# Value bias folded into other biases, value copies on ScalarE, low half of the scaled input by a negative identity, remote part transposed from its bank

## What is computed

```python
qkv = x @ qkv_w + qkv_b;  q, k, v = split(qkv)
local = windowed_attention(q, k, v)                   # 16 heads of 16, window of 128 earlier tokens
pooled = x.reshape(B, 64, 8, D).mean(2)               # 64 latent tokens
rq = x @ rq_w + rq_b;  rk, rv = split(pooled @ rkv_w + rkv_b)
lat_out = masked_attention(rq, rk, rv)                # 4 heads of 16, only earlier chunks
remote = lat_out @ rout_w + rout_b
gate = sigmoid(local @ gl_w + remote @ gr_w)          # one number per token and head
mixed = gate * local + (1 - gate) * remote
x = layernorm(x + mixed @ out_w + out_b)
h = gelu(rms_norm(x) @ ternary(w_up).T)
x = layernorm(x + rms_norm(h) @ ternary(w_down).T)
```

## Time and profile before

| what | us |
|---|---|
| runs shown, median (lowest, highest) of 3 | 1172.92 (1170.47, 1173.93) |
| the profiled execution, its time | 1173.3 |
| its span, first to last instruction | 1171.6 |
| TensorE busy | 982.2 |
| VectorE busy | 933.7 |
| POOL busy | 703.8 |
| ScalarE busy | 686.3 |
| mean granted clock of TensorE | 0.926 |

### The profile page before, as it was taken

How to read it: one execution, slowest core, us unless ns; L and a number is a source line. 1 busy time by engine, 2 the same in 40 slices (tenths; PEclk the granted TensorE clock), 3 DMA queues, 4 the chain that set the end, 5 groups by cost and what they waited for, 6 DMA issues and landing times. The chain is left out here.

```text
span 1171.6 us, 36746 instructions
## 1 busy us (share of the span) xinstructions
PE 982.2 (84%) x15202; PEld 634.5 (54%) x15202; DVE 933.7 (80%) x1928; ACT 686.3 (59%) x1093; POOL 703.8 (60%) x881
## 2 busy tenths in 40 slices
PE   5768898989988898998889898888988888884855
PEld 3445564656556565555646555565656555562523
DVE  6479879797988978798897979889897978875554
ACT  3424665657576565757656575756656576662544
POOL 7205765565667566566756656675665667673664
PEclk8879999999999999999999999999999999996787
DMA  7730604325070522507043340705234150601000
GB/s 220 204 103 27 172 30 120 100 66 154 5 215 4 153 67 75 144 4 216 3 136 83 86 134 4 216 4 163 57 101 119 48 153 4 187 16 37 1 20 18
DMA packets 58179, 107.50 MB, mean 92 GB/s; under 512 B 19718, under 2 KB 38038, under 8 KB 54934
## 3 DMA queue, kind: packets, MB, share of 16 engines
q1 hardware_dynamic: 57868, 105.15, 32.1%
q10 hardware_dynamic: 144, 0.00, 0.0%
HBM read 70.93 MB, written 33.55 MB: 89 GB/s over the span
## 5 line engine op out<-in xcount | busy, mean ns | idle before, releaser
L824 ACT ACTIVATE Pt<-scores 128x1024 f32<-128x1024 f32 (+1 forms) x256 | 230.0, 917 | 147.7 <-PE oacc L1508 83.7
L1091 DVE TENSOR_REDUCE nmax<-work 128x3 f32<-128x480 f32 x352 | 215.6, 634 | 37.0 <-PE work L1462 33.7
L677 POOL TENSOR_TENSOR h_lo<-hbuf,h_hi 128x512 f16<-128x512 f32 x128 | 148.0, 1156 | 157.4 <-DVE h_hi L1222 157.4
L649 POOL TENSOR_SCALAR_AFFINE_SELECT Pt<-Pt 128x512 f32<-128x512 f32 x256 | 164.1, 641 | 99.8 <-ACT Pt L824 99.2
L1508 PE MATMUL oacc<-Pt,Vp 128*32 128x256 f32 (+1 forms) x2048 | 155.7, 362 | 15.2 <-POOL Pt L653 8.5
L1457 PE MATMUL work<-Ks,Qs 98*32 98x160 bf16 x4096 | 150.4, 240 | 16.1 <-DVE nmax L1091 11.7
L636 POOL TENSOR_TENSOR parts<-Pt,parts 128x512 bf16<-128x512 f32 x64 | 72.9, 1158 | 136.0 <-ACT parts L749 136.0
L1488 PE MATMUL scores<-Qs,Ks 100*32 100x160 bf16 (+4 forms) x4096 | 126.9, 239 | 29.7 <-ACT Pt L824 14.1
L1521 PE MATMUL oacc<-wdn_t,h_hi 128*128 128x256 f16 x512 | 125.5, 283 | 18.0 <-POOL h_lo L677 18.0
L1488 PEld LDWEIGHTS scores<-Qs,Ks 100*32 100x32 bf16 x4096 | 87.8, 102 | 77.8 <-ACT Pt L824 47.6
L1521 PE MATMUL oacc<-wdn_t,h_lo 128*128 128x256 f16 x512 | 125.4, 283 | 0.0
(11 more groups left out here) (159 smaller groups left out, 1910.2 us busy)
## 6 DMA issues: line engine op xcount, KB each, us to landing
parts_scratch<-parts SPq DMA_DIRECT2D x96, 256.0 KB, 5.3
Qs<-parts_scratch SPq DMA_DIRECT2D x96, 256.0 KB, 5.1
Ks<-parts_scratch SPq DMA_DIRECT2D x96, 256.0 KB, 4.8
xT<-x_t SPq DMA_DIRECT2D x16, 512.0 KB, 6.7
xres<-x SPq DMA_DIRECT2D x16, 512.0 KB, 7.7
y<-nat SPq DMA_DIRECT2D x16, 512.0 KB, 3.1
Qs<-nmax_pair SPq DMA_DIRECT2D x256, 2.0 KB, 1.7
nat<-up_t SPq DMA_DIRECT2D x1, 1024.0 KB, 7.7
```

What stands on the lines that cost most here:

```text
L649: ins = pool.affine_select(out=pt[:, :, 0:P], in_=pt[:, :, 0:P], compare_op=ALU.is_gt, fill=0.0, base=0, pattern=[[0, 4], [1, P]], channel ...
L677: pool.tensor_tensor(h_lo[:, t % NR, :], hbuf[:, t % 2, :], h_hi[:, t % NR, :], ALU.subtract).then_inc(h_lo_ready, 1)
L824: nc.scalar.activation(Pt[:, u % NPT, :, 0:w], scores[:, slot, :, :].rearrange("p k (h q) -> p (k h) q", h=2)[:, :, 0:w], ACT.Exp, scale=S ...
L1091: nc.vector.tensor_reduce(nmax[:, first:first + n], work[:, slot, 0:n * BAND].rearrange("p (h c) -> p h c", h=n), X, ALU.max, negate=True) ...
```

## The change

1. The value bias is no longer added to the values. As the weights of a row sum to one, it adds the bias to the local output; it is taken out of both parts of the mix: `bout` gets the bias times the output weights added, and the remote part gets its own bias minus the value bias. The row without a key gets the negative bias through `dead`, which now has 18 columns. The values are then plain copies, done by ScalarE in VALUES+b.
2. The remote part is transposed by VectorE from its two banks; POOL adds its bias (`bias_remote`, two tensor_tensor of 128x512 per body, for the sequence after this one, behind the additions of `add_bias`).
3. The low half: TensorE's transposes of the scaled input stay open as a sum, a matmul with the negative identity `minus` (f16) subtracts the high half in the bank, and ScalarE copies the rest.
4. `split_maxima` moves from the first half to behind step UP+1 of the second (bodies 0 to 13; in body 14 it stays), and `move_max` on SP behind `restack`.
5. In the prologue: other and more weight loads, a few small instructions on VectorE and POOL, four small matmuls.

```diff
+SPLIT_AT = ("F", UP + 1)
...
-            (bv[:, :, :].rearrange("p h d -> p (h d)"), rows_of_all(v_b, H * VN)),
-            (brem[:, :], rout_b),
-            (brog[:, :], rout_bg),
-            (grc[:, :], gr_w),
+            (bv_col[:, :], bass.AP(v_b.tensor, v_b.offset, [[1, P], [P, KT]])),
+            (gcol[:, 0:1], gr_w),
+            (gcol[:, 1:2], gl_w),
+            (bog[:, 0, :], rout_bg),
+            (bog[:, 1, :], v_bg),
...
+        for c in range(4):
+            for q_tile, v in ((bv_q, v_b), (rem_b, rout_b)):
+                loads.append((q_tile[c * GT:(c + 1) * GT, :, :],
+                              bass.AP(v.tensor, v.offset + c * 2 * HD, [[0, GT], [P, KT], [1, 2 * HD]])))
...
 # SP, body
-                if not s.last:
+                if s.i == B - 2:
                     move_max(s.next())
                 if not s.first:
                     store_before(s)
                 if later.exists:
                     restack(later)
+                    move_max(s.next())
...
 # POOL
+            link(pool.tensor_scalar(minus[:, :], ident[:, :], -1.0, None, ALU.mult))
...
+            def bias_remote(s):
+
+                for i in range(2):
+                    bank, n = p_use(s, R_REM + i)
+                    pool.wait_ge(p_taken[bank], n + 1)
+                if s.first:
+                    pool.wait_ge(bias_ready, 1)
+                for t in range(KT):
+                    ins = pool.tensor_tensor(rem[:, s.par, t, :, :], rem[:, s.par, t, :, :],
+                                             rem_b[:, t, :].unsqueeze(1).to_broadcast([P, G32, 2 * HD]), ALU.add)
+                ins.then_inc(rem_biased, 1)
...
                 for b in range(NB):
                     add_bias(s, b)
+                if s.next().exists and not s.first:
+                    bias_remote(s.next())
...
 # ScalarE, p_step
+                if VALUES <= k < VALUES + NB:
+
+                    b = k - VALUES
+                    bank, n = p_use(s, R_V + b)
+                    act.wait_ge(p_full[bank], n + 1)
+                    of_heads = Vp[:, s.par, b, 0:H * VW].rearrange("p (h d) -> p h d", d=VW)
+                    nc.scalar.activation(of_heads[:, :, 0:VN],
+                                         p_bank(bank)[:, 0:H * VN].rearrange("p (h d) -> p h d", d=VN), ACT.Copy
+                                         ).then_inc(p_taken[bank], 1)
...
-                if k == REMOTE:
+                if k == REMOTE + 1:
 
                     if not s.first:
-                        act.wait_ge(rem_turned, count(s, 2, -1))
-                    for i in range(2):
-                        bank, n = p_use(s, R_REM + i)
-                        act.wait_ge(p_full[bank], n + 1)
-                        for t in range(KT):
-                            ins = nc.scalar.activation(remT[:, t, i * HALF:(i + 1) * HALF],
-                                                       p_bank(bank)[:, t * HALF:(t + 1) * HALF], ACT.Identity,
-                                                       bias=brem[:, t:t + 1])
-                        ins.then_inc(p_taken[bank], 1)
-                    act.wait_ge(p_taken[bank], n + 1)
-                    act.sem_inc(rem_copied, 1)
-                if k == REMOTE + 1:
-
+                        act.wait_ge(rem_turned, count(s, 1, -1))
...
 # ScalarE, f_step
+                if k == XN_LO:
+                    for t in range(KT):
+                        act.wait_ge(xn_rest, count(s, KT, t))
+                        nc.scalar.activation(xnT[:, 1, t, :], oacc[:, t, :], ACT.Copy).then_inc(xn_lo, 1)
...
 # VectorE, p_step
-                def take_values(b):
-                    bank, n = take(R_V + b)
-                    of_heads = Vp[:, s.par, b, 0:H * VW].rearrange("p (h d) -> p h d", d=VW)
-                    nc.vector.tensor_tensor(of_heads[:, :, 0:VN],
-                                            p_bank(bank)[:, 0:H * VN].rearrange("p (h d) -> p h d", d=VN),
-                                            bv[:, :, :], ALU.add).then_inc(p_taken[bank], 1)
-
-                if VALUES <= k < VALUES + NB and (k != VALUES + 1 or s.i < 2):
-                    take_values(k - VALUES)
-                if k == LAT_EXP + 1 and s.i >= 2:
-                    take_values(1)
...
                 if k == REMOTE:
-                    dve.wait_ge(rem_copied, count(s, 2, 0))
-                    for t in range(KT):
-                        ins = nc.vector.transpose(rem[:, s.par, t, :, :].rearrange("p b d -> p (b d)"), remT[:, t, :])
-                    ins.then_inc(rem_turned, 1)
+                    for i in range(2):
+                        bank, n = take(R_REM + i)
+                        nc.vector.transpose(rem[:, s.par, :, i * G32 // 2:(i + 1) * G32 // 2, :],
+                                            p_bank(bank).rearrange("p (t b d) -> p t b d", t=KT, d=GT)
+                                            ).then_inc(p_taken[bank], 1)
...
 # VectorE, f_step
-                    done(nc.vector.tensor_tensor(a, of_heads[:, :, VN],
-                                                 dead[:, :, :, :].rearrange("p t b m -> p (t b m)"), ALU.add))
-                    done(nc.vector.reciprocal(r, a))
+                    done(nc.vector.tensor_tensor(o_q[:, :, 0, :, 0:VW], o_q[:, :, 0, :, 0:VW], dead[:, :, :, :],
+                                                 ALU.add))
+                    done(nc.vector.reciprocal(r, of_heads[:, :, VN]))
...
+                    dve.wait_ge(rem_biased, count(s, 1, 0))
...
-                if k == XN_LO:
-                    for t in range(KT):
-                        dve.wait_ge(xn_hi, count(s, KT, t))
-                        nc.vector.tensor_tensor(xnT[:, 1, t, :], oacc[:, t, :], xnT[:, 0, t, :], ALU.subtract
-                                                ).then_inc(xn_lo, 1)
...
 # VectorE, body
-                    if u == A_STEPS and not s.last:
-                        split_maxima(s.next())
+                if s.i == B - 2:
+                    split_maxima(s.next())
...
+                    if (phase, k) == SPLIT_AT and s.i < B - 2:
+                        split_maxima(s.next())
...
 # TensorE, f_step
-                            mm = nc.tensor.transpose(oacc[:, t, b * P:(b + 1) * P],
-                                                     xn[:, b, t * P:(t + 1) * P], ident[:, :])
+                            mm = nc.tensor.matmul(oacc[:, t, b * P:(b + 1) * P], xn[:, b, t * P:(t + 1) * P],
+                                                  ident[:, :], is_transpose=True, start=(b == 0), stop=False,
+                                                  skip_group_check=True)
...
+                if k == XN_LO:
+                    for t in range(KT):
+                        pe.wait_ge(xn_hi, count(s, KT, t))
+                        nc.tensor.matmul(oacc[:, t, :], minus[:, :], xnT[:, 0, t, :], start=False, stop=True,
+                                         skip_group_check=True).then_inc(xn_rest, 1)
```

More of the change, by code:

```diff
@@ L701, in add_bias @@
                     pool.wait_ge(xres_in, count(s, 1, 0) * 16)
+                if b == 0 and s.first:
+                    pool.wait_ge(bias_ready, 1)
                 pool.tensor_tensor(xres[:, b, :], xres[:, b, :], bout[:, :], ALU.add).then_inc(xres_done, 1)
@@ L929, in prepare @@
                 wro3 = wro[:, :].rearrange("p (h d) -> p h d", h=H)
-                for w3, o in [(wv[:, t, :, 0:HD], wv[:, t, :, HD:VN]) for t in range(KT)] + \
-                             [(bv[:, :, 0:HD], bv[:, :, HD:VN])]:
+                dve.wait_ge(consts, 3)
+                dead3 = dead[:, :, :, :].rearrange("p t m d -> p (t m) d")
+                bv3 = bv_q[:, :, :].rearrange("p t (m d) -> p (t m) d", m=2)
+                few = ytok[:, 1, 0:KT * 2 * HD].rearrange("p (h d) -> p h d", d=HD)
+                link(nc.vector.tensor_scalar(dead3[:, :, 0:HD], bv3, -1.0, None, ALU.mult))
+                link(nc.vector.tensor_tensor(few, dead3[:, :, 0:HD], gl3[:, 0:KT * 2, :], ALU.mult))
+                link(nc.vector.tensor_reduce(dead3[:, :, HD:VN], few, X, ALU.add))
+                link(nc.vector.tensor_scalar(dead3, dead3, first_row[:, :], None, ALU.mult))
+                nc.vector.tensor_tensor(rem_b[:, :, :], rem_b[:, :, :], bv_q[:, :, :], ALU.subtract)
+                dve.wait_ge(gate_bias, 1)
+                link(nc.vector.tensor_tensor(bout[:, :], bout[:, :], oacc[:, 0, 0:D], ALU.add))
+                dve.sem_inc(bias_ready, 1)
+                for w3, o in [(wv[:, t, :, 0:HD], wv[:, t, :, HD:VN]) for t in range(KT)]:
                     link(nc.vector.tensor_tensor(tmp, w3, gl3, ALU.mult))
@@ L1503, in weigh @@
                     pe.wait_ge(o_taken, count(s, HG, hg - 2))
+                if s.first and v == 0:
+                    pe.wait_ge(bias_ready, 1)
+                    pe.wait_ge(gate_bias, 2)
                 pe.wait_ge(masked, count(s, NU, v))
```

59 lines of the change are left out of this document (36 added, 23 removed).

## The result

The changed kernel takes 1230.88 us (median of 4, 1228.86 to 1231.45); the kernel before, run beside it, 1171.7 (1167.72 to 1173.93). The ratio is **1.051** (95% interval 1.047 to 1.054). Slower was right; the size was not. The forecast was +36 us, measured are +59, and the time lies 7 us above the range.

What follows compares the result with a forecast made beforehand. Three queues (VectorE, ScalarE, TensorE) were taken to bound the body in turn. Bodies 1 to 13 add 13 x (1.4 + 0.9) = 29.9 us, body 0 0.9, body 14 2.5, body 15 1.1, prologue 1: +35.4, so 1208 us, range 1178 to 1224.

Steps and rivals of the forecast that it cites:

- The block at the gate: Gate stretch: VectorE's two-input instructions wait for POOL's tensor_tensor, including new ones; +1.4 us per body, ends -0.6 and +1.9.
- Everything after hangs on this chain, so the term goes through: Behind the gate: mixT, output product and norm hang on the gate chain, so its +1.4 us passes on.
- Norm to GELU: From the norm to the first GELU: ScalarE's value and low-half copies delay table load and GELU; +1.25 us, lower end +0.6.
- The split: Behind GELU, before L1074: the moved maxima split, less one value copy, adds 0.75 us towards the third tile's h_hi.
- The tail: End of the body: ScalarE's four remote copies and VectorE's wait for them vanish; -1.1 us per body.
- Rows of maxima: Maxima DMAs on SP: issued till 287, 5.6 us left before the next scores; rival, rows land late: 1231, chance 0.05.
- Prologue: Prologue: longer weight list and more VectorE instructions against a vanished wait of the remote transposes; +1 us, ends -3 and +6.
- Last bodies: Bodies 14 and 15: ScalarE's low-half copies delay GELU 1.1 us, body 14 also has POOL's pair; +2.5 and +1.1 us.
- POOL doesn't hold VectorE: Rival at the gate: POOL's two new additions fall into VectorE's waits, or POOL waits; 1186 us, chance 0.2.
- VectorE alone paces: Rival, from L1140 to the ones-column product: VectorE alone paces the body and gets faster; 1152 us, chance 0.15.

Runs made afterwards that it cites:

- filled: Changed kernel with 14 matmuls that feed nothing ahead of TensorE's output product, POOL's pair of bias additions left in place: 1197.75 us, ratio 1.026.
- pair_filled: Kernel before plus two unused POOL tensor_tensor of 128x512 at the gate and 14 useless matmuls ahead of the output product: 1190.39 us, ratio 1.019.
- pair_late: Changed kernel with POOL's two bias additions waiting until both halves of mixT are there: 1180.16 us, ratio 1.008.
- late_low_split_b: Changed kernel with POOL's bias additions waiting for mixT, low half on VectorE again, maxima split and its DMAs back in the first half: 1154.1 us, ratio 0.987.
- before_bank: Kernel before with the remote part transposed from its banks, without ScalarE's four copies and with its bias left out: 1144.45 us, ratio 0.976.
- before_single_b: Kernel before plus four unused POOL tensor_scalar of 128x512 with one SBUF input at the gate: 1190.2 us, ratio 1.015.
- the gains of pair and low half: Changed kernel with POOL's additions waiting for mixT (51 us gained), or low half on VectorE again (31 us gained); both together 1160.27 us.
- one part of it alone: Kernel before with only the remote part turned from its banks, its bias added by POOL behind mixT: 1146.47 us, ratio 0.980.

## Why the prediction was right in sign and wrong in size

- **The block at the gate: right mechanism, undersized.** I took +1.4 us, between -0.6 and +1.9. Measured are 2.0 (2.08 less 0.09). I had L1143 wait for the fourth residual addition and only L1148 meet the new instructions. In the trace the fourth addition ends under the reciprocal, and both new instructions hold VectorE in full (at L1177 and L1182, which were L1143 and L1148), so the upper end was the reading to take. The addition of `dead`, which I had at no extra cost, takes 0.86 us instead of 0.71 besides (body 2). By the Trainium skill's rule (SBUF, section Who interferes with whom, under Practical consequences) taken strictly the term was 1.9; for two-input instructions of both engines the runs agree with it.
- **"Everything after hangs on this chain, so the term goes through": the step that failed.** It let a delay pass at size one. Nothing in my sum asked what TensorE does meanwhile. It idles 3.14 us instead of 1.16, is granted 1.2 GHz, and the product takes 1.7 us longer. ScalarE's parts, POOL's subtractions and the powers behind them in POOL's list follow, and the second nbias is 1.1 us late on top of the gate's delay. With the idle filled and the gate still held the way from mixT to nbias is back at 12.98 (`filled`) and 13.09 us (`pair_filled`), 13.02 in the kernel before. Over 13 bodies this term, which the sum had at nothing, is 15 us. Of the 23 missing it is the largest: the gate adds 8 and the way from norm to GELU 13, while split and tail give back 12. The Trainium skill (TensorE: Matmul & The Clock Gate, section HAM oscillation — how this bites in real kernels) describes waits that recur in each iteration and leave each burst of matmuls behind them at the lower clock; 3.68 against 2.00 us agrees, and I hadn't weighed it.
- **Norm to GELU: +1.25 forecast, +2.3 measured; the second step that failed.** The part up to nbias was right: where the product runs at full clock (`pair_late`) the first nbias comes 1.06 us sooner and the second no sooner. The mis-sized terms are TensorE's: the two negative-identity matmuls at 0.22 us each, and the value product at 0.9, were full-clock prices for matmuls that stand right behind an idle of 1.32 us, and I put the value product behind them without seeing that ScalarE's table load then waits for it. With the order swapped it is 1.25. The two numbers meet in part by luck, as the forecast had the other order and TensorE's terms at full clock.
- **The split: +0.75 forecast, +0.36 measured** in the body; 6 us of the whole in `late_low_split_b`, where it is clear of noise. The attention instruction L1107 behind it takes 1.22 us, and took 1.45 in its old place (L1074).
- **The tail: -1.1 forecast, -0.9 measured.** What I missed is 0.75 us more behind the ones column. `before_bank` shows that it comes with the remote part. Part of it goes with the clock: in this stretch the kernel before spends 2.6 us per body at 1.2 GHz, and the changed kernel and `before_bank` none (over the whole span 175 us in 33 stretches fell to 96 in 14 in `before_bank`). But the three bodies of the kernel before without it still take 24.4 us there, so the rest is not explained, and no run shows which wait let the clock fall.
- **Rows of maxima:** their 16 issues run from 288.36 for 10.03 us, and no body between 1 and 13 waits for them, as forecast. **Prologue:** +1.7 against +1, the first half of body 0 included. **Last bodies:** +3.6 forecast, +0.8 measured. In body 14 TensorE waits 11.7 us for the maxima rows of the last sequence, as before (11.8), and the gate's delay lies inside that wait.
- **Rivals.** "POOL doesn't hold VectorE" fell with L1177 at 1.27 us; "VectorE alone paces" fell with GELU 30.46 us after the last value matmul (24.78 before) while VectorE waited 5.45 us for it. The reason I gave for the first, that POOL's `tensor_scalar` holds nothing, is wrong too: in `before_single_b` it costs 0.4 us an instruction. No rival had the clock in it, so the range ended too low.

Three things stay open. Why the gains of pair and low half add to 71 and not 82 us is only in part accounted for, and no run holds the clock fixed in both. Whether the low half on ScalarE could pay at all was tried only in the two orders above. And the fill was not run on the kernel before.

## What to carry to other kernels

The price of work moved to POOL was here neither its duration nor POOL's share but what it held: put a two-input POOL instruction where VectorE has no two-SBUF-input work of the chain (here behind mixT: 37 us for one wait). Look at TensorE's idle ahead of each short product on the chain, and at the granted clock over it; a delay that lengthened it from 1.2 to 3.1 us was paid again by the clock here. And time the parts of a change one by one: the whole was 5.1% slower, one part of it alone is 2.0% faster.

## What the runs showed of the hardware that was not expected

- Fourteen useless matmuls of 3.2 us made the kernel 33 us faster. Some 15 of them are the way from mixT to nbias, with the output product at 1.99 us instead of 3.68.
- A POOL `tensor_scalar` of 128x512 takes 1.57 us in the mean, longer than the `tensor_tensor` at 1.16 to 1.27, but costs a VectorE gate instruction only about 0.4 us. L1147 starts 0.06 us after it and takes 0.65 us, where the `tensor_tensor` made it wait to its end; L1154 starts 0.95 us after it and takes 0.62. L1154 is a VectorE `tensor_scalar` with one input (0.19 us in the kernel before). The Trainium skill (SBUF, section Who interferes with whom) lets the one that starts first keep the port for its whole instruction; for two-input instructions the runs agree, for this one they don't.
- Turning the remote part from its banks gave 30 us, where I had counted 15 for the copies and waits removed; with them went the stretch at the lower clock that ten of 13 bodies had in their first half. That this is the cause of the other 15 us isn't shown.
